# Sparse expert lookup of a graph network: groups of two gathers in a ring of eight, and a search spread over two tiles

## The chip, the cores and the metric

The kernel runs on one core of one Trainium2 chip. The metric is the device time in microseconds (us) of that core for one execution; less is better. TensorE is called PE here, VectorE DVE, ScalarE ACT, GpSimd POOL and SyncE SP.

## The reference, cut to what matters

The input x has 1250 rows of 512 floats. Four layers follow each other, each adding its result to x: a graph convolution with batch norm and GELU, a product-key expert lookup, a second graph convolution, and a binned dense layer. The change lies in the second layer, and in the start of the third that runs beside it:

```python
y = layernorm(x)                                  # 1250 x 512
q = (y @ Wq + bq).reshape(-1, 8, 128)             # 8 heads, two halves of 64
s1 = einsum(q[..., :64], keys[:, 0]); s2 = einsum(q[..., 64:], keys[:, 1])   # 256 scores each
s1t, i1 = top_k(s1, 8); s2t, i2 = top_k(s2, 8)
scores, best = top_k(all 64 sums of s1t and s2t, 8)
indices = the 8 pairs i1 * 256 + i2               # 64 rows of the tables for each row of y
vals = relu(einsum(y, w_down[indices])) * softmax(scores)
x = x + einsum(vals, w_up[indices])
```

Each of the 1250 rows of x so needs 64 rows of `w_down` and 64 of `w_up`. The host has put both tables side by side, so one gathered row has 1024 floats, 4096 bytes. All floats are fp32.

## The kernel before, in words

The rows of x are in NT = 10 tiles of 128 rows, one row to a partition. Before the lookup, the first graph layer runs; after it, the rest of the third layer and the sorted dense layer. The lookup and what runs beside it take most of the time.

**A slot.** For one tile and one of its 64 chosen experts, POOL issues an indirect DMA (line 476) that brings 128 table rows, one to each partition, into a slot of `big`. There are 16 slots. They are handled in groups of GS = 4, so NG = 16 groups a tile, and the ring has RING = 4 groups. A group passes four engines:

1. POOL waits until PE is done with the group that had these slots before (`grp_done`, line 471; also `val_ready`, line 470), then issues four gathers.
2. DVE waits until the group has landed, and forms four dot products of the `w_down` halves with y (line 956). After a drain it takes relu and multiplies by the softmax weight `prob` (line 961) for the four together, which gives `val`.
3. ACT makes four diagonal matrices `diag` from the identity, scaled by `val` (line 642).
4. PE multiplies them with the `w_up` halves and accumulates all 64 in one PSUM bank (line 1274). This sets `grp_done`. One fp32 matmul shows as two records.

**The search for the next tile** runs in between, in pieces tied to group numbers, written out by hand for each engine (`pieces` in the functions of PE, ACT and DVE). While tile i passes, DVE takes the norm of tile i + 1 (lines 822 to 840) at groups 1 and 2, PE transposes it at 2 (line 1221), PE computes the queries of four heads at group 3 and of four at 4 (line 1230), ACT copies them out at 4 and 5 (line 621), PE makes the scores of two heads in each of the groups 5 to 8 (line 1243), and DVE takes their eight best in groups 6 to 9, two heads at a time (lines 856 and 859). The pairs follow at 10 (lines 868 to 875), the row numbers are ready at 12 (line 902), the softmax at 14. Each engine does its list in order: an engine that waits in a piece does nothing for the ring meanwhile.

**The third layer's sums.** The finished tile i - 1 is added to x (line 922), normalized (line 840), and multiplied with the adjacency counts `AT` in 12 units (line 1253), two for each of the groups 10 to 15; DVE adds each unit to `outT` one group later (line 849). The units go alternately to two PSUM banks.

```python
pieces = {2: flip_y, 3: lambda i, p: queries(i, 0), 4: lambda i, p: queries(i, 1),
          5: lambda i, p: scores(i, 0), 6: lambda i, p: scores(i, 2), 7: lambda i, p: scores(i, 4),
          8: lambda i, p: scores(i, 6)}                      # PE
pieces = {1: root, 3: copy_yT, 4: lambda i: copy_q(i, 0), 5: lambda i: copy_q(i, 1), 12: exps}   # ACT
```

POOL and ACT run the tiles in loops of two tiles (ACT its first eight tiles, POOL all ten); DVE and PE have tiles 0, 1, 8 and 9 written out and a loop of two tiles for 2 to 7.

## Time and profile before

| what | value |
|---|---|
| time, median of 3 runs | 1517.33 us |
| lowest and highest run | 1516.46 and 1520.87 us |
| span of the profiled execution | 1598.9 us |
| time of the profiled execution apart from its span | not given; the span is the only one |
| mean granted clock of PE | 0.914 |
| instructions | 17228 |

The profile is of one execution, and its span is 81.6 us longer than the median of the runs without a profile. A row of a group gives line, engine, operation, the tiles written and read and how many; then its busy time, the mean of one in ns, and the idle time of the engine just before, with what ended it. In a timeline the first two numbers are the start and the duration in us; a merged row covers several instructions. A clock of 1.00 is 2.4 GHz, 0.50 is 1.2 GHz. The ends of matmuls are modelled.

### The profile page before, as it was taken

The numbers are of one execution on the slowest core, as the hardware profiler recorded it, in microseconds if no ns is written. First come the engines' busy times: TensorE is split into PE (matmuls) and PEld (weight loads), VectorE is DVE, ScalarE is ACT, GpSimd is POOL, SyncE is SP. The second block draws the span as 40 slices with busy tenths as digits, with TensorE's granted clock in tenths as the row PEclk, the third lists the DMA queues.
The fourth block names the chain that finished last, engine by engine and source line by source line (L and its number), as shares of the span: only waits on it lengthen the run. The fifth ranks groups of instructions, "written<-read, shape, count | busy, mean of one in ns | idle before, by whom it ended". The sixth has DMA issues, their size and how long they took to land.

```text
span 1598.9 us, 17228 instructions
## 1 busy us (share of the span) xinstructions
PE 1246.5 (78%) x3954; PEld 604.1 (38%) x3955; DVE 979.1 (61%) x3058; ACT 335.6 (21%) x910; POOL 829.4 (52%) x921
## 2 busy tenths in 40 slices
PE   4787789974877877797778878867887878788468
PEld 1333345542422433444334334343343433233233
DVE  4777771127497586684864866747758678555501
ACT  0111110024322223232221222221222222220011
POOL 5777700002567566565555665655656656763112
PEclk9999999985899999899888989988989999999779
DMA  9200000003889889898888898887998989986153
GB/s 350 87 0 0 0 0 0 1 0 118 307 305 349 298 325 345 281 324 320 302 302 301 300 336 301 316 322 261 361 338 291 354 301 350 373 327 243 72 184 125
DMA packets 105746, 378.51 MB, mean 237 GB/s; under 512 B 11824, under 2 KB 11826, under 8 KB 104536
## 3 DMA queue, kind: packets, MB, share of 16 engines
q0 software_dynamic: 94720, 343.40, 59.3%
q1 hardware_dynamic: 10968, 34.48, 5.8%
q8 instruction: 19, 0.31, 0.1%
q14 instruction: 39, 0.32, 0.1%
HBM read 359.53 MB, written 19.41 MB: 237 GB/s over the span
## 4 chain that ended last, share of the span: by engine, by line
PE 47%; DVE 19%; issue 12%; ACT 5%; DVEq 5%; another core or an unknown queue 5%; DMA 5%; POOL 2%; POOLq 0%; SPq 0%; ACTq 0%
PE tr L1274 20%; DVE big L956 8%; PE acc L1171 5%; PE acc L1230 4%; PE acc L1131 4%; PE acc L1253 3%; PE tr L1326 2%; DVE topi L859 2%; DMA big<-in_wdu,idx 2%; ACT diag L642 2%; PE tr L1302 2%; PE acc L1201 2%; PE acc L1243 2%; DVEq L730 2%
## 5 line engine op out<-in xcount | busy, mean ns | idle before, releaser
L476 POOL DMA_INDIRECT big<-in_wdu,idx x640 | 641.8, 1003 | 587.0 <-issue 583.1
L1274 PE MATMUL tr<-big,diag 128*128 128x512 f32 x1280 | 650.1, 656 | 190.2 <-ACT diag L642 98.1
L956 DVE CUSTOM_DVE_ANT_0 big<-big,y 128x512 f32<-128x512 f32 x640 | 405.3, 689 | 129.9 <-DMA big<-in_wdu,idx 100.9
L1274 PEld LDWEIGHTS tr<-big,diag 128*128 128x128 f32 x1280 | 255.8, 209 | 536.4 <-issue 402.2
L642 ACT ACTIVATE diag<-ident,val 128x128 f32<-128x128 f32 x640 | 204.6, 393 | 604.7 <-DVE val L961 342.1
L1131 PE MATMUL acc<-outT 128*128 128x512 f16 (+1 forms) x612 | 126.1, 345 | 33.0 <-POOL outT L461 14.7
L461 POOL TENSOR_SCALAR outT<-gt,big 128x128 f16<-128x128 f16 x153 | 130.2, 864 | 21.8 <-PE acc L1131 10.9
L856 DVE MAX8 top<-acc 128x8 f32<-128x256 f32 x160 | 61.2, 424 | 109.8 <-PE acc L1243 97.9
L736 DVE TENSOR_SCALAR outT<-big 128x1250 f16<-128x1250 f16 x204 | 110.3, 595 | 17.6 <-PE acc L1131 12.1
L1230 PE MATMUL acc<-yT,qk 128*128 128x128 f32 x640 | 86.5, 301 | 25.3 <-ACT qT L621 24.7
L1253 PE MATMUL acc<-AT,gt 128*128 (+2 forms) x240 | 97.4, 529 | 4.2 <-DVE gt L840 3.2
L849 DVE TENSOR_TENSOR outT<-outT,acc 128x512 f32<-128x512 f32 (+1 forms) x120 | 67.1, 586 | 54.4 <-PE acc L1253 37.6
L1230 PEld LDWEIGHTS acc<-yT,qk 128*128 128x128 f32 x640 | 85.0, 216 | 36.8 <-issue 19.3
L1131 PEld LDWEIGHTS acc<-outT 128*128 128x128 f16 x612 | 50.3, 98 | 106.7 <-DVE outT L736 36.8
L1171 PE MATMUL acc<-AT,big 128*128 128x512 f32 (+1 forms) x240 | 87.1, 526 | 3.8 <-DVEq L767 3.8
L1253 PEld LDWEIGHTS acc<-AT,gt 128*128 128x128 f32 x240 | 46.0, 195 | 56.1 <-issue 46.0
L859 DVE FIND_INDEX8 topi<-top,acc 128x8 uint32<-128x256 f32 x160 | 65.9, 424 | 1.2 <-issue 1.2
L1171 PEld LDWEIGHTS acc<-AT,big 128*128 128x128 f32 x240 | 46.7, 195 | 43.8 <-issue 39.7
L956 DVE DVE_READ_ACCUMULATOR2_ANT inner<- 128x1 f32 x640 | 52.6, 82 | 0.0
L621 ACT ACTIVATE qT<-acc,par 128x128 f32<-128x128 f32 x80 | 22.9, 369 | 139.1 <-remote 79.6
L1243 PE MATMUL acc<-qk,qT 64*128 64x256 f32 x320 | 47.5, 414 | 4.8 <-DVEq L861 4.4
L1079 DVE TENSOR_SCALAR pick<-x 128x1 int32<-128x1 f32 x14 | 2.2, 154 | 74.1 <-PE tr L1326 74.1
(217 smaller groups left out, 782.1 us busy)
## 6 DMA issues: line engine op xcount, KB each, us to landing
sorted_rows<-big SPq DMA_DIRECT2D x8, 1280.0 KB, 17.9
big<-in_wdu,idx POOLq DMA_INDIRECT x640
big<-in_we SPq DMA_DIRECT2D x8, 1024.0 KB, 14.0
x<-sorted_rows SPq DMA_DIRECT2D x14, 512.5 KB, 3.5
x<-in_x SPq DMA_DIRECT2D x1, 2304.0 KB
...
```

The costliest lines, as they stand in the source:

```text
L461: pool.tensor_scalar(k.ohd[c], k.tile_iota, k.dnow[:, c:c + 1], None, ALU.is_equal).then_inc(k.ohd_ready, 1)
L476: pool.indirect_dma_start(out=k.big[:, slot * 2 * D:(slot + 1) * 2 * D], out_offset=None, in_=k.wdu_d, in_offset=bass.IndirectOffsetOnAxis ...
L642: ins = act.activation(k.diag[:, ((g % 2) * GS + s) * P:((g % 2) * GS + s + 1) * P], k.ident[:, :], copy, scale=k.val[:, j:j + 1])
L736: dve.tensor_scalar(k.ohs[c][:, 0:N], k.iota[:, 0:N], k.now[:, c:c + 1], None, ALU.is_equal).then_inc(k.oh_ready, 1)
L859: ins = dve.max_index(k.topi[:, c * HK + h * 8:c * HK + h * 8 + 8], k.top[:, c * HK + h * 8:c * HK + h * 8 + 8], k.S[h % 2][c][:, 0:NK])
L956: dve.tensor_tensor_reduce(out=k.big[:, slot:slot + D], in0=k.big[:, slot:slot + D], in1=k.y[:, par * D:(par + 1) * D], scale=1.0, scalar=0.0,
L1131: ins = pe.matmul(k.acc[s][:, c0:c0 + n], k.ohd[b], k.ohs[b][:, c0:c0 + n], start=False, stop=False)
L1171: ins = pe.matmul(k.acc[s][:, c0:c0 + n], h[:, t * D + f * P:t * D + (f + 1) * P], k.AT[:, t * NPAD + c0:t * NPAD + c0 + n], start=(t == 0 ...
L1230: ins = pe.matmul(k.Q[:, b * P:(b + 1) * P], k.wq[:, f * H * P + h * P:f * H * P + (h + 1) * P], k.yT[:, f * P:(f + 1) * P], start=(f == 0 ...
L1243: ins = pe.matmul(k.S[h % 2][c][:, 0:NK], k.qT[half, h * P:(h + 1) * P], k.keys[half, h * NK:(h + 1) * NK], start=True, stop=True)
L1253: pe.matmul(k.G[u % 2][:, 0:n], k.h1[:, f * P:(f + 1) * P], k.AT[:, bass.ds(j * NPAD + c0, n)], start=True, stop=True).then_inc(k.g_ready, 1)
L1274: ins = pe.matmul(k.O[par], k.diag[:, c:c + P], k.big[:, slot:slot + D], start=(g == 0 and s == 0), stop=(g == NG - 1 and s == GS - 1))
```

## The change

It has four parts.

- **Two gathers a group.** GS is 2, NG is 32, RING is 8; there are still 16 slots. POOL no longer waits for DVE's semaphore, only for `grp_done`. There are four `diag` sets of two.
- **The softmax weight as the product's scale.** The dot product takes `prob` as its scale from memory, so the drain and the small product of line 961 are gone; ACT makes the diagonals with Relu in place of Copy.
- **The search in single steps over two tiles.** The search for tile j starts at step -14 (18 groups into tile j - 2) and ends at step 15 of tile j - 1. One step is one group of two. Queries are made for two heads at a time, scores and top eights for one. DVE takes a head two or more steps after PE made its scores. The search for tile 1 is shifted by 11 steps. y has three buffers.
- **Units one by one.** PE makes one unit in every second group from 8 on, in one PSUM bank in place of two, and DVE adds it three groups later. The transposed y moves to the bank of the queries. The norms of y and of the finished x are apart, with semaphores of their own.

All loops over tiles are written out: the engines have ten tiles of code each. The work after the lookup is unchanged.

```diff
-GS = 4
+GS = 2
 NG = HK // GS
-RING = 4
+RING = 8
+DB = 4
...
-UPP = 2
-FIRST_UNIT = NG * UPP - len(UNITS)
+NU = len(UNITS)
+
+
+Y_STATS, Y_NORM = -14, -11
+HEADS = (-4, -3, -1, 0, 2, 3, 5, 6)
+BEST, PLACE, CODES, MATCH, ROWS, INDEX, SOFTMAX = 8, 9, 10, 11, 12, 13, 15
+Y_ROOT, Y_FLIP, Y_COPY = -13, -10, -9
+QUERIES = (-9, -7, -5, -3)
+Q_COPY = (-8, -6, -4, -2)
+SCORES = (-6, -5, -3, -2, 0, 1, 3, 4)
+EXPS = 12
+LATE = 11
+
+
+X_ADD, X_STATS, X_ROOT, X_NORM = 4, 5, 6, 7
+UNIT_MM = [8 + 2 * u for u in range(NU)]
+UNIT_ADD = [11 + 2 * u for u in range(NU)]
+
+
+def at_search(i, g):
+
+    return [(i + a, g - NG * (a - 1) - (LATE if i + a == 1 else 0)) for a in (1, 2) if i + a < NT]
...
-    k.y = sb("y", 2 * D)
+    k.y = sb("y", 3 * D)
...
-    k.diag = sb("diag", 2 * GS * P)
+    k.diag = sb("diag", DB * GS * P)
...
-    k.YT = banks[0]
+    k.YT = banks[1]
...
-    def gather_tile(i, par):
-
+    for i in range(NT):
         pool.wait_ge(k.idx_ready, i + 1)
         for g in range(NG):
             r = g % RING
-
-            pool.wait_ge(k.val_ready, i * NG + g + 1)
             pool.wait_ge(k.grp_done, i * NG + g + 1)
-            pool.sem_inc(k.ring_free, 1)
             for s in range(GS):
                 j = g * GS + s
                 slot = r * GS + s
                 pool.indirect_dma_start(
                     out=k.big[:, slot * 2 * D:(slot + 1) * 2 * D], out_offset=None, in_=k.wdu_d,
-                    in_offset=bass.IndirectOffsetOnAxis(ap=k.idx[par][:, j:j + 1], axis=0),
+                    in_offset=bass.IndirectOffsetOnAxis(ap=k.idx[i % 2][:, j:j + 1], axis=0),
                 ).then_inc(k.landed[r], 16)
-
-    with pool.Fori(0, NT // 2) as pair:
-        gather_tile(pair * 2, 0)
-        gather_tile(pair * 2 + 1, 1)
...
+    def tile(i):
         for g in range(NG):
-            if g in pieces and (ahead or g == 1):
-                pieces[g](i + 1)
-            act.wait_ge(k.val_ready, i * NG + g + 1 + RING)
-            act.wait_ge(k.grp_done, i * NG + g - 1 + RING)
+            if i and g == X_ROOT:
+                x_root(i - 1)
+            for j, at in at_search(i, g):
+                search_step(j, at)
+            n = i * NG + g
+            act.wait_ge(k.inner_ready, n + 1)
+            act.wait_ge(k.grp_done, n + 1 - DB + RING)
             for s in range(GS):
                 j = g * GS + s
-                ins = act.activation(k.diag[:, ((g % 2) * GS + s) * P:((g % 2) * GS + s + 1) * P], k.ident[:, :],
-                                     copy, scale=k.val[:, j:j + 1])
+                c = (n % DB) * GS + s
+                ins = act.activation(k.diag[:, c * P:(c + 1) * P], k.ident[:, :], ACT.Relu,
+                                     scale=k.inner[:, j:j + 1])
             ins.then_inc(k.diag_ready, 1)
...
+    def x_add(i):
+        dve.wait_ge(k.grp_done, i * NG + NG + RING)
+        tile = k.x[:, i * D:(i + 1) * D]
+        dve.tensor_tensor(tile, tile, k.O[i % 2], ALU.add).then_inc(k.x2_done, 1)
...
+    def add_unit(j, u, bank):
+        f, c0, n = UNITS[u]
+        piece = k.agg1[:, f * NPAD + c0:f * NPAD + c0 + n]
+        dve.wait_ge(k.g_ready, j * NU + u + 1)
+        dve.tensor_tensor(piece, piece, k.G[bank][:, 0:n], ALU.add).then_inc(k.g_used, 1)
+
+    def top_head(i, h):
+        dve.wait_ge(k.s_ready, i * H + h + 1)
+        dve.sem_inc(k.s_seen, 1)
+        for c in range(2):
+            dve.max(k.top[:, c * HK + h * 8:c * HK + h * 8 + 8], k.S[h % 2][c][:, 0:NK])
+        dve.drain()
+        for c in range(2):
+            dve.max_index(k.topi[:, c * HK + h * 8:c * HK + h * 8 + 8],
+                          k.top[:, c * HK + h * 8:c * HK + h * 8 + 8], k.S[h % 2][c][:, 0:NK])
+        dve.drain().then_inc(k.topk_done, 1)
...
+    def tile(i):
         for g in range(NG):
-            if g == 1:
-                if behind:
-                    add_rows(i - 1, 1 - par)
-                norms(i + 1, ahead, behind)
-            if g == 2:
-                normed(i + 1, 1 - par, ahead, behind)
-            if ahead and g in pieces:
-                pieces[g](i + 1, 1 - par)
-            if behind and g > NG - len(UNITS) // UPP:
-                add_units(i - 1, (g - 1) * UPP - FIRST_UNIT, UPP)
-            if first_tile and g in (3, 4):
-                for t in range((g - 3) * (NT // 2), (g - 2) * (NT // 2)):
-                    loops = k.AT[:, t * NPAD + t * P:t * NPAD + (t + 1) * P]
-                    dve.tensor_tensor(loops, loops, k.ident[:, :], ALU.subtract)
-            if first_tile and g >= NG - FT:
+            if i and g == X_ADD:
+                x_add(i - 1)
+            if i and g == X_STATS:
+                x_stats(i - 1)
+            if i and g == X_NORM:
+                x_norm(i - 1)
+            if i and g in UNIT_ADD:
+                add_unit(i - 1, UNIT_ADD.index(g), 0)
+            if i > 1 and g + NG in UNIT_ADD:
+                add_unit(i - 2, UNIT_ADD.index(g + NG), 0)
+            for j, at in at_search(i, g):
+                search_step(j, at)
+            if i == 0 and g < NT:
+                loops = k.AT[:, g * NPAD + g * P:g * NPAD + (g + 1) * P]
+                dve.tensor_tensor(loops, loops, k.ident[:, :], ALU.subtract)
+            if i == 0 and g >= NG - FT:
                 dve.memset(k.agg1[:, (g - NG + FT) * NPAD:(g - NG + FT + 1) * NPAD], 0.0)
+            n = i * NG + g
             r = g % RING
-            use = i * (NG // RING) + g // RING
-            dve.wait_ge(k.landed[r], use * (16 * GS) + 16 * GS)
+            dve.wait_ge(k.landed[r], (n // RING + 1) * (16 * GS))
             for s in range(GS):
+                j = g * GS + s
                 slot = (r * GS + s) * 2 * D
-                dve.tensor_tensor_reduce(out=k.big[:, slot:slot + D], in0=k.big[:, slot:slot + D],
-                                         in1=k.y[:, par * D:(par + 1) * D], scale=1.0, scalar=0.0,
-                                         op0=ALU.mult, op1=ALU.add,
-                                         accum_out=k.inner[:, g * GS + s:g * GS + s + 1])
-            dve.drain()
-            dve.scalar_tensor_tensor(k.val[:, g * GS:(g + 1) * GS], k.inner[:, g * GS:(g + 1) * GS], 0.0,
-                                     k.prob[:, par * HK + g * GS:par * HK + (g + 1) * GS],
-                                     ALU.max, ALU.mult).then_inc(k.val_ready, 1)
-        if behind:
-            add_units(i - 1, len(UNITS) - UPP, UPP)
-
-    dve.sem_inc(k.val_ready, RING)
-    dve.sem_inc(k.g_used, 2)
-    search(0, 0)
+                ins = dve.tensor_tensor_reduce(
+                    out=k.big[:, slot:slot + D], in0=k.big[:, slot:slot + D],
+                    in1=k.y[:, (i % 3) * D:(i % 3 + 1) * D],
+                    scale=k.prob[:, (i % 2) * HK + j:(i % 2) * HK + j + 1], scalar=0.0, op0=ALU.mult, op1=ALU.add,
+                    accum_out=k.inner[:, j:j + 1])
+            ins.then_inc(k.inner_ready, 1)
...
+    def queries(i, c):
         pe.wait_ge(k.yT_done, i + 1)
-        pe.wait_ge(k.qT_done, i * H + 4 * half)
-        for b in range(4):
-            h = 4 * half + b
+        pe.wait_ge(k.qT_done, i * H + 2 * c)
+        for h in (2 * c, 2 * c + 1):
             for f in range(FT):
-                ins = pe.matmul(k.Q[:, b * P:(b + 1) * P], k.wq[:, f * H * P + h * P:f * H * P + (h + 1) * P],
+                ins = pe.matmul(k.Q[:, (h % 4) * P:(h % 4 + 1) * P],
+                                k.wq[:, f * H * P + h * P:f * H * P + (h + 1) * P],
                                 k.yT[:, f * P:(f + 1) * P], start=(f == 0), stop=(f == FT - 1))
         ins.then_inc(k.q_ready, 1)
 
-    def scores(i, h0):
-        for h in (h0, h0 + 1):
-            pe.wait_ge(k.qT_done, i * H + h + 1)
-            if h >= 2:
-                pe.wait_ge(k.topk_done, i * H + h - 1)
-            else:
-                pe.wait_ge(k.topk_done, i * H)
-            for c in range(2):
-                half = slice(64 * c, 64 * c + 64)
-                ins = pe.matmul(k.S[h % 2][c][:, 0:NK], k.qT[half, h * P:(h + 1) * P],
-                                k.keys[half, h * NK:(h + 1) * NK], start=True, stop=True)
-            ins.then_inc(k.s_ready, 1)
-
-    def units(j, u0, n_units):
-
+    def scores(i, h):
+        pe.wait_ge(k.qT_done, i * H + h + 1)
+        pe.wait_ge(k.topk_done, max(i * H + h - 1, 0))
+        for c in range(2):
+            half = slice(64 * c, 64 * c + 64)
+            ins = pe.matmul(k.S[h % 2][c][:, 0:NK], k.qT[half, h * P:(h + 1) * P],
+                            k.keys[half, h * NK:(h + 1) * NK], start=True, stop=True)
+        ins.then_inc(k.s_ready, 1)
+
+    def unit(j, u, bank, ahead):
+        f, c0, n = UNITS[u]
         pe.wait_ge(k.ht_ready, j + 1)
-        for u in range(u0, u0 + n_units):
-            f, c0, n = UNITS[u]
-            pe.wait_ge(k.g_used, j * len(UNITS) + u + 1)
-            pe.matmul(k.G[u % 2][:, 0:n], k.h1[:, f * P:(f + 1) * P], k.AT[:, bass.ds(j * NPAD + c0, n)],
-                      start=True, stop=True).then_inc(k.g_ready, 1)
-
-    pieces = {2: flip_y, 3: lambda i, p: queries(i, 0), 4: lambda i, p: queries(i, 1),
-              5: lambda i, p: scores(i, 0), 6: lambda i, p: scores(i, 2), 7: lambda i, p: scores(i, 4),
-              8: lambda i, p: scores(i, 6)}
-
-    def search(i, par):
-        for g in (2, 3, 5, 4, 6, 7, 8):
-            pieces[g](i, par)
-
-    def tile(i, par, ahead, behind):
+        pe.wait_ge(k.g_used, max(j * NU + u - ahead, 0))
+        pe.matmul(k.G[bank][:, 0:n], k.h1[:, f * P:(f + 1) * P], k.AT[:, j * NPAD + c0:j * NPAD + c0 + n],
+                  start=True, stop=True).then_inc(k.g_ready, 1)
+
+    def search_step(i, at):
+        if at == Y_FLIP:
+            flip_y(i)
+        if at in QUERIES:
+            queries(i, QUERIES.index(at))
+        if at in SCORES:
+            scores(i, SCORES.index(at))
+
+    def tile(i):
         for g in range(NG):
-            if ahead and g in pieces:
-                pieces[g](i + 1, 1 - par)
-            if behind and g >= NG - len(UNITS) // UPP:
-                units(i - 1, g * UPP - FIRST_UNIT, UPP)
-            pe.wait_ge(k.diag_ready, i * NG + g + 1)
+            for j, at in at_search(i, g):
+                search_step(j, at)
+            if i and g in UNIT_MM:
+                unit(i - 1, UNIT_MM.index(g), 0, 0)
+            n = i * NG + g
+            pe.wait_ge(k.diag_ready, n + 1)
             for s in range(GS):
                 slot = ((g % RING) * GS + s) * 2 * D + D
-                c = ((g % 2) * GS + s) * P
-                ins = pe.matmul(k.O[par], k.diag[:, c:c + P], k.big[:, slot:slot + D],
+                c = ((n % DB) * GS + s) * P
+                ins = pe.matmul(k.O[i % 2], k.diag[:, c:c + P], k.big[:, slot:slot + D],
```

## Rows read from the trace of the kernel before

**Rows 1.** The page, part 1: busy time of each engine over the whole span.
```profile
span 1598.9 us, 17228 instructions
...
PE 1246.5 (78%) x3954; PEld 604.1 (38%) x3955; DVE 979.1 (61%) x3058; ACT 335.6 (21%) x910; POOL 829.4 (52%) x921
```

**Rows 2.** Windows: stretch, us, busy PE, PEld, DVE, ACT, POOL, clock, DMA share, GB/s.
```profile
612.00:718.00 106.00, 86.13 (x254) 42.67 (x255) 75.89 (x253) 29.48 (x83) 63.45 (x65) 0.92 0.89 316
...
1254.00:1360.00 106.00, 86.97 (x259) 41.69 (x260) 75.84 (x253) 27.49 (x80) 65.08 (x65) 0.94 0.92 331
...
384.00:1446.00 1062.00, 843.55 (x2428) 405.09 (x2428) 723.01 (x2419) 272.83 (x791) 641.81 (x640) 0.91 0.88 316
```

**Rows 3.** The page, part 3: the queue that carries the gathers.
```profile
q0 software_dynamic: 94720, 343.40, 59.3%
```

**Rows 4.** The page, part 5: the lookup's groups, with the idle time before them.
```profile
L476 POOL DMA_INDIRECT big<-in_wdu,idx x640 | 641.8, 1003 | 587.0 <-issue 583.1
L1274 PE MATMUL tr<-big,diag 128*128 128x512 f32 x1280 | 650.1, 656 | 190.2 <-ACT diag L642 98.1
L956 DVE CUSTOM_DVE_ANT_0 big<-big,y 128x512 f32<-128x512 f32 x640 | 405.3, 689 | 129.9 <-DMA big<-in_wdu,idx 100.9
```

**Rows 5.** Timeline of gathers: start, duration, idle before; the last two are tile 9's.
```profile
606.02 0.95 POOL L476 DMA_INDIRECT big<-in_wdu,idx  x1 [0.30 <-issue]
...
648.76 0.95 POOL L476 DMA_INDIRECT big<-in_wdu,idx  x1 [5.41 <-issue]
...
1341.71 0.95 POOL L476 DMA_INDIRECT big<-in_wdu,idx  x1 [0.77 <-issue]
...
1431.70 0.95 POOL L476 DMA_INDIRECT big<-in_wdu,idx  x1 [0.30 <-issue]
```

**Rows 6.** Windows of 5 us in tiles 1 and 2: full and starved DMA engines.
```profile
590.00:595.00 5.00, 5.00 (x12) 2.18 (x12) 2.77 (x12) 1.28 (x4) 3.60 (x4) 1.00 1.02 416
...
645.00:650.00 5.00, 5.00 (x18) 2.20 (x17) 1.17 (x4) 1.86 (x7) 0.95 (x1) 1.00 0.39 155
```

**Rows 7.** Timeline: group 3 of tile 2 through the ring.
```profile
617.11 0.95 POOL L476 DMA_INDIRECT big<-in_wdu,idx  x1 [0.30 <-issue]
...
623.98 0.69 DVE L956 CUSTOM_DVE_ANT_0 big<-big,y 128x512 f32<-128x512 f32 x1 [2.31 <-DMA big<-in_wdu,idx]
...
626.60 0.16 DVE L961 SCALAR_TENSOR_TENSOR val<-inner,prob 128x4 f32<-128x4 f32 x1
...
626.80 1.28 ACT L642 ACTIVATE diag<-ident,val 128x128 f32<-128x128 f32 x4 [2.39 <-DVE val L961]
...
630.62 3.60 PE L1274 MATMUL tr<-big,diag 128*128 128x512 f32 x8
```

**Rows 8.** Waits between 384 and 1446 us: who for whom, total us, times, longest us.
```profile
DVE top L856 <- PE acc L1243: 87.3, 18, 10.0
ACT qT L621 <- remote: 79.6, 8, 12.3
...
DVE outT L849 <- PE acc L1253: 30.7, 32, 3.0
```

**Rows 9.** Timeline of DVE in tile 3: two heads of one piece, and their second waits.
```profile
760.99 0.76 DVE L856 MAX8 top<-acc 128x8 f32<-128x256 f32 x2
...
763.03 0.76 DVE L856 MAX8 top<-acc 128x8 f32<-128x256 f32 x2 [0.30 <-issue]
```

**Rows 10.** Timeline of PE: queries, a unit pair, and a group at the lower clock.
```profile
607.04 1.40 PE L1253 MATMUL acc<-AT,gt 128*128 128x512 f32 x4
...
627.05 3.73 PE L1230 MATMUL acc<-yT,qk 128*128 128x128 f32 x32
...
732.73 6.38 PE L1274 MATMUL tr<-big,diag 128*128 128x512 f32 x8 [5.72 <-ACT diag L642]
```

**Rows 11.** Groups with shapes apart: the score product and ScalarE's table loads.
```profile
L961 DVE SCALAR_TENSOR_TENSOR val<-inner,prob 128x4 f32<-128x4 f32 x160 | 26.2, 164 | 23.3 <-issue 11.6
...
L626 ACT ACT_TABLE_LOAD x10 | 12.8, 1283 | 0.2
```

More of the change, by code:

```diff
@@ new lines, in softmax, with search_step @@
+        dve.drain()
+    def search_step(i, at):
+        if at == Y_STATS:
+            y_stats(i)
+        if at == Y_NORM:
+            y_norm(i)
+        if at in HEADS:
+            top_head(i, HEADS.index(at))
+        if at == BEST:
+            best()
+        if at == PLACE:
+            place()
+        if at == CODES:
+            codes()
+        if at == MATCH:
+            match()
+        if at == ROWS:
+            rows()
+        if at == INDEX:
+            index(i)
+        if at == SOFTMAX:
+            softmax(i)
@@ L984, in dve_program @@
-    add_units(NT - 1, 0, len(UNITS))
+    dve.drain()
+    for at in range(Y_STATS, -LATE):
+        search_step(1, at)
+    for i in range(NT):
+        tile(i)
+    for u in range(NU):
+        if UNIT_ADD[u] >= NG:
+            add_unit(NT - 2, u, 0)
+    x_add(NT - 1)
+    x_stats(NT - 1)
+    x_norm(NT - 1)
+    for u in range(NU):
+        add_unit(NT - 1, u, u % 2)
     dve.drain()
@@ L1280, in pe_program @@
     pe.sem_inc(k.grp_done, RING)
-    search(0, 0)
+    for at in range(Y_FLIP, SCORES[-1] + 1):
+        search_step(0, at)
     for i in range(1, NT):
@@ L1284, in pe_program @@
     pe.wait_ge(k.x1_done, NT)
[L1285 to L1295 removed]
+    for i in range(NT):
+        tile(i)
+    for u in range(NU):
+        unit(NT - 1, u, u % 2, 0 if u == 0 else 1)
+    pe.wait_ge(k.g_used, NT * NU)
     pe.wait_ge(k.x2_done, NT)
```

176 lines of the change are left out of this document (69 added, 107 removed).

## The prediction

> **What bounds the kernel now.** I read the page's totals first: no engine is full over the span of 1598.9 us, PE with 78% comes nearest [rows 1]. Then the windows over the lookup, which holds two thirds of the span: 1062 us in which PE is busy 843.6, DVE 723.0, POOL 641.8 and the DMA engines 88% [rows 2]. A tile takes 106 or 107 us in them, whether it lies in the written-out loops or not. So the question is what each engine would need for one tile if nothing held it up.
>
> POOL: a gather takes 1.003 us on average [rows 4], and the next starts 0.30 us later when nothing holds POOL [rows 5]. 64 x 1.303 = 83.4 us a tile. DMA: the gathers' queue moved 343.40 MB [rows 3], 0.537 MB each; full engines move 416 GB/s [rows 6], so 1.29 us a gather and 82.6 us a tile. PE: 86.1 us busy in a tile at a granted clock of 0.92 [rows 2], about 79 us at the full one. DVE: 75.9 us busy [rows 2], plus what the busy time leaves out, a 0.30 us wait after each drain of a head [rows 9], 16 of them a tile: about 81 us. Four engines need 79 to 83 us each, and the tile takes 106. From 384 to tile 9's first gather at 1341.7 [rows 2, 5] nine tiles take 957.7 us, 106.4 each. POOL's part of that is 83.4, so it stands 23.0 us a tile waiting for a slot. A long stand is seen at 648.76, after 5.41 us [rows 5], and the DMA engines were at 0.39 share and 155 GB/s around it [rows 6]. The kernel is bound by its hand-overs, not by an engine.
>
> Two hand-overs matter. **The ring's own length:** group 3 of tile 2 is fully issued at 618.06; its products start at 623.98, 5.9 us later, with DVE waiting for the DMA; the value is ready at 626.76, 2.8 us later; the diagonals take 1.28 us, and the matmuls 3.60 us, which here start late [rows 7]. With 5.0 us to issue four gathers and 0.3 us to start again, a group needs 5.0 + 5.9 + 2.8 + 1.3 + 3.6 + 0.3 = 18.9 us from first issue to reuse. The ring gives it four groups' time at POOL's pace, 4 x 4 x 1.303 = 20.8 us. Less than 2 us of lateness on any engine stops POOL. **The search:** DVE waits 87.3 us for score matmuls, up to 10.0 us at a time, 30.7 us for units, and ACT 79.6 us for the queries, up to 12.3 us [rows 8]. Each far exceeds 2 us. The 12.3 us ones end on a release that the profile can't name.
>
> **The change, part by part.** Groups of two: 2.5 to issue, 5.9 to land, about 1.5 for two products, 0.7 for two diagonals, 1.8 for the matmuls, 0.3: 12.7 us of the same 20.8, so 8.1 us of slack in place of 1.9. The cost is 16 more starts of a group on each engine. No row shows that start alone; from 0 to the 0.30 us of a drained wait [rows 9], 0 to 4.8 us a tile. I take 1.6, because nothing is drained there any more.
>
> The value product: 26.2 us over 160 [rows 11], 2.6 us a tile of DVE, goes, and with it a hand-over on each group's way. The scale read from memory instead of a constant isn't in the trace. The same product at 0.689 us [rows 4] bounds it below; above I allow a tenth, 0.07 x 64 = 4.5 us a tile. I take nothing: 512 elements pass either way. DVE so needs 81 - 2.6 + 1.6 = 80 us, up to 88 at both upper bounds. Relu in place of Copy on ACT: at worst a table load of 1.283 us [rows 11] around each change of function, a few us a tile, under ACT's idle time (29.5 of 106 us busy [rows 2]); that cover is ample.
>
> The search in steps: queries in four parts of 16 matmuls, half of a record row of 3.73 us [rows 10], so PE is away from the ring for 1.9 us at a time, less than the slack. DVE takes one head of 2.04 us [rows 9] at a time, two steps after PE made it, so the 87.3 us of waits should mostly go; likewise the 30.7 us for units, now added three groups later. PE's unit waits for the add of the one before, because one bank is left; that add, 0.6 us, lies beside ACT's diagonals. What becomes late next is DVE's uneven list: steps 0 to 9 hold five heads (10.2 us), ten products of two (about 14) and some 7.5 us of norms, adds and pairs, 31.7 us against the 10 x 2.6 = 26.1 that POOL takes; it falls 5.6 us behind, within 8.1, and catches up in steps 16 to 27, which hold little. PE's steps 23 to 30 (units, queries and scores together) are about as tight. The softmax and row numbers are ready at steps 15 and 13, well ahead of their first use. POOL's extra waits are on `grp_done` alone, two gathers queued behind each.
>
> **The sum.** Tile 9 has no search at all: its 64 gathers run from 1341.7 to 1432.7 [rows 5], 90.9 us, 7.5 us over POOL's 83.4. I take that residue and 1.5 us for the uneven list: 92.4 us a tile. Nine tiles save 9 x (106.4 - 92.4) = 126 us, tile 9 about 2, the rest of the program nothing: its search, tail and layers issue the same work. The profiled span would be 1598.9 - 128 = 1471 us.
>
> The runs without a profile are 81.6 us shorter than that span, and where these lie I can't see. If they are spread in proportion, the saving is 128 x 1517.33 / 1598.9 = 121 us and the time 1396. If they all lie in the nine tiles (the 79.6 us of unnamed releases [rows 8] suggest it), an unprofiled tile already takes 97.3 us, the saving is 9 x 4.9 + 2 = 46, and the time 1471. The truth is between; I take 1430.
>
> A rule speaks against the change. Mean gathers take 1.003 us, usual ones 0.95 [rows 4, 5], so 0.05 us each is lost to something now. The Trainium skill (SBUF - State Buffer, "Who interferes with whom") says that a DVE instruction with two SBUF inputs contends with a GpSimd one that reads SBUF, and that one blocks wholly. The row shows only a mean of 0.05 us for it, if it is that. By the rule the denser stream of products could block POOL more often; that is the second rival.
>
> **The rivals.** (1) The residue goes too: all engines run at their need, 84 us a tile; 9 x 22.4 = 202 us of the span, 191 in proportion, 1326. For: four needs of 79 to 83. Against: four engines so evenly filled never all run freely, and tile 9 doesn't. Chance 0.07. (2) POOL is held up: if half of the products' 0.689 us fell on each gather, 64 x 0.34 = 22 us a tile would take back the 23.0 that POOL stood, and the time stays near 1517. Against: the 0.05 us now. Chance 0.05. (3) Slower: PE's clock. After 5.72 us of idleness a group took 6.38 us instead of 3.60 [rows 10, 7], at the lower level. Now PE gets 1.8 us of work at a time and waits twice as often. Its 79 us become the bound of 106 below a mean clock of 0.74; at 0.70 a tile is 113 us, 9 x 6.6 x 0.95 = 56 us more, 1573. Against: shorter stands, with more work per us than now, and 0.92 today. Chance 0.09. In the TensorE: Matmul & The Clock Gate page of the Trainium skill ("What's actually happening") the throttled state is the default and activity releases it; by that, steadier work helps. (4) The waits only move, from heads to other steps: 100 us a tile, 1517.3 - 9 x 6.4 x 0.95 = 1463; that lies in my forecast.
>
> **The numbers.** The forecast, with (4), has 0.79. A measurement of this kernel tells 0.3%, 4.6 us, from no change. Faster 0.86 (0.79 + 0.07), same 0.05, slower 0.09. The range goes from 1365 (88.5 us a tile in proportion) to 1500 (the span's excess all in the tiles and DVE near 88 with waits left), which leaves out (1), (2) and (3).
>
> **What would show it.** Right: POOL's idle time falls from 587 us by some 130, beside a gather mean still near 1.0; DVE's wait for scores falls under 20 us; the lookup's windows show 360 GB/s or more, PE's clock 0.92 or better, a tile of about 92 us. Wrong: DVE's group of line 956 with a mean over 0.75; gathers over 1.1 us; a clock under 0.8; DVE waits on steps 0 to 9 that fill the ring.

## The result and the profile after

The changed kernel takes **1434.89 us** (median of four runs, 1433.85 to 1435.95) against 1517.78 us for the kernel before, four runs on the same chip: a ratio of 0.9455, 95% interval 0.9438 to 0.9471. The forecast was 1430 in a range of 1365 to 1500.

The profiled execution of the changed kernel lasts 1434.2 us. Its totals, its gather queue and its costliest groups (busy us, mean ns | idle us before, and the releaser of most of it):

```profile
span 1434.2 us, 16301 instructions
...
PE 1201.3 (84%) x3954; PEld 565.9 (39%) x3955; DVE 989.3 (69%) x2906; ACT 345.7 (24%) x914; POOL 857.4 (60%) x921
...
q0 software_dynamic: 94720, 343.40, 62.6%
...
L493 POOL DMA_INDIRECT big<-in_wdu,idx x640 | 670.1, 1047 | 396.2 <-DVE idx L931 180.7
L1302 PE MATMUL tr<-big,diag 128*128 128x512 f32 x1280 | 612.0, 607 | 85.9 <-ACT diag L666 85.6
L992 DVE CUSTOM_DVE_ANT_0 big<-big,y,prob 128x512 f32<-128x512 f32 x640 | 451.1, 747 | 76.1 <-DMA big<-in_wdu,idx 63.8
...
L883 DVE MAX8 top<-acc 128x8 f32<-128x256 f32 x160 | 60.9, 422 | 69.9 <-PE acc L1272 68.7
```

These answer to [rows 1, 3, 4] and the first of [rows 8]. The ring's matmuls wait 85.9 us in place of 190.2, the value product's group is gone, and POOL's idle time is 396.2 in place of 587.0; 180.7 of it is the wait for the first row numbers, ahead of the lookup. (A second profile of the kernel before, below, has 167.7 and 509.0 for these two.) Two rows went the wrong way: a gather takes 1.047 us in place of 1.003, and a product 0.747 in place of 0.689.

A window of 700 us, nearly eight steady tiles, and four gathers of the timeline; the first and the last are the first gathers of tiles 0 and 9:

```profile
480.00:1180.00 700.00, 631.73 (x1949) 293.05 (x1948) 596.08 (x1863) 217.90 (x614) 529.07 (x501) 1.00 0.99 376
```
```profile
384.25 1.22 POOL L493 DMA_INDIRECT big<-in_wdu,idx  x1 [180.70 <-DVE idx L931]
...
580.60 1.43 POOL L493 DMA_INDIRECT big<-in_wdu,idx  x1 [0.95 <-PE tr L1302]
...
614.59 1.87 POOL L493 DMA_INDIRECT big<-in_wdu,idx  x1 [0.74 <-PE tr L1302]
...
1188.38 1.01 POOL L493 DMA_INDIRECT big<-in_wdu,idx  x1 [0.30 <-issue]
```

Nine tiles take 1188.38 - 384.25 = 804.1 us, **89.35 us each**. PE's granted clock is 1.00, the DMA engines are busy 99% of the time at 376 GB/s, and POOL issues nearly without a pause: its waits for a slot are now about a microsecond, as in the second row. The third row is a gather that itself took twice the usual time; that is taken up with the second SBUF operand below. The same shows in the waits between 384 and 1280 us (who for whom, total us, times, longest us):

```profile
ACT diag L666 <- DVE inner L992: 466.1, 245, 3.7
...
POOL big L493 <- issue: 171.7, 563, 0.5
...
DVE top L883 <- PE acc L1272: 55.9, 26, 7.0
POOL big L493 <- PE tr L1302: 43.8, 76, 1.7
```

POOL's "issue" time is the fixed 0.30 us between gathers, 563 times and never over 0.5; its waits for the ring's matmuls last 1.7 us at most. In [rows 5] one lasted 5.41.

### The profile page after: what moved, and what is told of

It reads as the page before. It is cut to its first block, busy times and chain, and to the rows that moved or that the text cites. A ratio compares the mean times of both kernels' runs of the same rounds, so it can differ in the third digit from the quotient of the medians.

```text
span 1434.2 us, 16301 instructions
## 1 busy us (share of the span) xinstructions
PE 1201.3 (84%) x3954; PEld 565.9 (39%) x3955; DVE 989.3 (69%) x2906; ACT 345.7 (24%) x914; POOL 857.4 (60%) x921
## 4 chain that ended last, share of the span: by engine, by line
PE 47%; DVE 28%; issue 6%; DVEq 6%; DMA 5%; POOL 3%; ACT 3%; POOLq 0%; SPq 0%; ACTq 0%
PE tr L1302 17%; DVE big L992 11%; PE acc L1204 6%; PE acc L1262 5%; PE acc L1164 5%; PE acc L1280 4%; DVE topi L886 4%; POOL big L493 3%; PE tr L1351 3%; DVE top L883 2%; DMA big<-in_wdu,idx 2%; PE tr L1327 2%; PE acc L1234 2%; DVEq L752 2%; DVE outT L758 1%
## 5 line engine op out<-in xcount | busy, mean ns | idle before, releaser
L493 POOL DMA_INDIRECT big<-in_wdu,idx x640 | 670.1, 1047 | 396.2 <-DVE idx L931 180.7
L1302 PE MATMUL tr<-big,diag 128*128 128x512 f32 x1280 | 612.0, 607 | 85.9 <-ACT diag L666 85.6
L992 DVE CUSTOM_DVE_ANT_0 big<-big,y,prob 128x512 f32<-128x512 f32 x640 | 451.1, 747 | 76.1 <-DMA big<-in_wdu,idx 63.8
L1302 PEld LDWEIGHTS tr<-big,diag 128*128 128x128 f32 x1280 | 229.5, 190 | 391.3 <-issue 216.6
L666 ACT ACTIVATE diag<-ident,inner 128x128 f32<-128x128 f32 x640 | 219.5, 394 | 466.1 <-DVE inner L992 466.1
L1164 PE MATMUL acc<-outT 128*128 128x512 f16 (+1 forms) x612 | 125.8, 344 | 33.5 <-POOL outT L482 15.5
L758 DVE TENSOR_SCALAR outT<-big 128x1250 f16<-128x1250 f16 x204 | 109.9, 592 | 17.9 <-PE acc L1164 12.3
L1280 PE MATMUL acc<-AT,gt 128*128 128x512 f32 (+1 forms) x240 | 108.3, 537 | 12.5 <-DVE outT L877 7.3
L1262 PEld LDWEIGHTS acc<-yT,qk 128*128 128x128 f32 x640 | 80.6, 199 | 20.8 <-issue 18.8
L1262 PE MATMUL acc<-yT,qk 128*128 128x128 f32 x640 | 81.8, 283 | 1.8 <-ACT qT L637 1.0
L1280 PEld LDWEIGHTS acc<-AT,gt 128*128 128x128 f32 x240 | 41.4, 191 | 75.5 <-issue 71.3
L1272 PE MATMUL acc<-qk,qT 64*128 64x256 f32 x320 | 57.9, 440 | 4.4 <-DVEq L888 4.4
```

Source lines behind the costliest of these rows:

```text
L493: pool.indirect_dma_start(out=k.big[:, slot * 2 * D:(slot + 1) * 2 * D], out_offset=None, in_=k.wdu_d, in_offset=bass.IndirectOffsetOnAxis ...
L666: ins = act.activation(k.diag[:, c * P:(c + 1) * P], k.ident[:, :], ACT.Relu, scale=k.inner[:, j:j + 1])
L758: dve.tensor_scalar(k.ohs[c][:, 0:N], k.iota[:, 0:N], k.now[:, c:c + 1], None, ALU.is_equal).then_inc(k.oh_ready, 1)
L992: ins = dve.tensor_tensor_reduce(out=k.big[:, slot:slot + D], in0=k.big[:, slot:slot + D], in1=k.y[:, (i % 3) * D:(i % 3 + 1) * D], scale= ...
L1164: ins = pe.matmul(k.acc[s][:, c0:c0 + n], k.ohd[b], k.ohs[b][:, c0:c0 + n], start=False, stop=False)
L1262: ins = pe.matmul(k.Q[:, (h % 4) * P:(h % 4 + 1) * P], k.wq[:, f * H * P + h * P:f * H * P + (h + 1) * P], k.yT[:, f * P:(f + 1) * P], sta ...
```

## The experiments

All runs in one table. "us/tile" is the start of tile 9's first gather less that of tile 0's, over 9. "Stands" is what POOL waits beyond 0.30 us between gathers, per tile, in those nine tiles. Ratios are to runs of the kernel before on the same chip; its medians there were 1518.54 (beside e2 to e4), 1520.18 (e5 to e8), 1517.88 (e9 to e11) and 1516.39 (e12). They lie 4 us apart, so a difference of a few us between rows of different chips is uncertain by about as much.

| run | us, median (lowest to highest) | ratio [95% interval] | us/tile | gather, us | product, us | stands |
|---|---|---|---|---|---|---|
| before, profile shown | 1517.78 (1516.46-1520.87) | 1 | 106.4 | 1.003 | 0.689 | 22.7 |
| e1_base | 1517.9 (one) | | 98.35 | 0.998 | 0.689 | 14.9 |
| e2_scale | 1516.97 (1510.72-1521.84) | 0.9987 [0.9968, 1.0005] | 97.7 | 1.013 | 0.748 | 13.4 |
| e3_pairs | 1480.75 (1478.6-1481.56) | 0.9757 [0.9724, 0.9789] | 94.2 | 1.051 | 0.690 | 7.2 |
| e4_pairs_scale | 1460.79 (1458.34-1463.65) | 0.962 [0.9583, 0.9656] | 92.2 | 1.023 | 0.748 | 7.1 |
| e8_pairs_scale_unrolled | 1445.25 (1443.32-1446.4) | 0.9501 [0.9452, 0.9551] | 90.2 | 1.033 | 0.748 | 4.4 |
| **after** | 1434.89 (1433.85-1435.95) | 0.9455 [0.9438, 0.9471] | 89.35 | 1.047 | 0.747 | 2.3 |
| e5_after_fours | 1512.26 (1508.12-1518.42) | 0.9957 [0.9932, 0.9982] | 97.1 | 1.007 | 0.747 | 13.2 |
| e11_unrolled | 1495.04 (1494.58-1498.41) | 0.9846 [0.9808, 0.9884] | 95.6 | 1.000 | 0.689 | 12.0 |
| e6_after_unit_scale | 1418.41 (1416.79-1420.52) | 0.9331 [0.9281, 0.9381] | 87.3 | 1.020 | 0.689 | 2.2 |
| e7_after_narrow | 1388.71 (1384.97-1390.66) | 0.9138 [0.9089, 0.9187] | 83.45 | 0.961 | 0.282 | 2.4 |
| e9_one_score | 1435.05 (1431.68-1435.83) | 0.9446 [0.9412, 0.948] | 88.5 | 1.043 | 0.746 | 1.8 |
| e10_y_in_psum | 1429.25 (1428.41-1432.2) | 0.9412 [0.9376, 0.9448] | 87.8 | 0.953 | 0.741 | 7.3 |
| **e12_weight_on_act** | 1419.45 (1417.23-1420.43) | 0.9357 [0.9329, 0.9385] | 86.6 | 0.952 | 0.681 | 6.1 |

### The kernel before, profiled again

The profile on which the prediction rests had a span 81.6 us over the timed runs. Run e1_base is the same kernel.

> The kernel before, unchanged, profiled once more. The first profile of it had a span of 1598.9 us against runs of 1517 us, with 79.6 us of ACT waits at line 621 on a release that the profile couldn't name; the changed kernel's profile (span 1434.2 us) has neither. Theory A (the excess belongs to recording this kernel): the span is again near 1599 us and the 79.6 us are there. Theory B (that one execution was disturbed): the span is near 1517 us, a tile takes about 97 us in the windows, and POOL's idle time before line 476 is some 80 us below 587 us.

The new profile's span is 1516.1 us (timeline rows first, then the page's group of gathers and waits between 384 and 1250 us):

```profile
383.32 1.22 POOL L476 DMA_INDIRECT big<-in_wdu,idx  x1 [179.87 <-issue]
...
1268.45 0.94 POOL L476 DMA_INDIRECT big<-in_wdu,idx  x1 [0.78 <-issue]
...
1350.30 0.94 POOL L476 DMA_INDIRECT big<-in_wdu,idx  x1 [0.31 <-issue]
```
```profile
L476 POOL DMA_INDIRECT big<-in_wdu,idx x640 | 638.8, 998 | 509.0 <-issue 504.8
```
```profile
ACT qT L621 <- PE acc L1230: 69.1, 18, 5.3
...
DVE top L856 <- PE acc L1243: 45.0, 15, 5.4
```

It agrees with the timed runs to 2 us. Nine tiles take 885.1 us, 98.35 each, and the releases that the first profile couldn't name don't appear. So the first profile was of an unusual execution, and its 81.6 us lay mainly in the nine tiles: 9 x (106.4 - 98.35) = 72. Another 8 us lay in tile 9: from its first gather to the end of its last, 1268.45 to 1351.24, it takes 82.8 us here, where the first profile had the 90.9 from which the prediction took its residue. The waits for queries and scores were there in ordinary executions too, but at most 5.4 us long rather than 12.3. What disturbed that one execution stays open. From here on "before" means e1_base; the change is worth 9 x (98.35 - 89.35) = 81 of the 83 us measured.

### One part at a time: weight as scale, groups of two

```diff
 e2_scale: before, and
-  tensor_tensor_reduce(..., scale=1.0, ...); dve.drain(); scalar_tensor_tensor(k.val, ...)
+  tensor_tensor_reduce(..., scale=k.prob[:, j], ...)      # diagonals: Relu(ident * inner)
 e3_pairs: before, and
-GS = 4; RING = 4
+GS = 2; RING = 8; DB = 4       # search pieces stay at every fourth gather
 e4_pairs_scale: both
```

> Part two alone on the kernel before: the softmax weight as the product's scale, Relu, no drain and no product of the four values. Groups of four and the old search stay. Ring-length theory: the way of a group through the ring shortens by about 0.25 us of 18.9, but each product takes 0.747 us in place of 0.689 as in the changed kernel, four of them 0.23 us more; so nothing, 1512 to 1522 us. Rival (the value product and its hand-over cost much): below 1500 us.

> Part one alone on the kernel before: groups of two, eight in the ring, four diag sets of two; each piece of the search still stands at the same place of the tile, two heads at once, units in pairs on two banks, the value product kept. Ring-length theory: the slack grows from 1.9 to about 8 us, which covers most stands but not the 10 us waits for scores; about half of the gain, 1465 to 1490 us. Search theory: the waits of the search stay whole, so nothing or less than 10 us, 1507 to 1520 us.

> Parts one and two on the kernel before, without the search in single steps over two tiles. What is left to the changed kernel's 1435 us is the worth of the steps. Ring-length theory: 1460 to 1485 us, so the steps are worth 25 to 50 us. Search theory: 1500 to 1520 us, so the steps are worth 65 to 85 us.

The product in the kernel with the scale alone:

```profile
L957 DVE CUSTOM_DVE_ANT_0 big<-big,y,prob 128x512 f32<-128x512 f32 x640 | 443.3, 748 | 125.7 <-DMA big<-in_wdu,idx 106.8
```

Alone, the scale is worth nothing that can be measured: the interval holds 1. What the value product and its drain gave, the longer product (+59 ns) took. Groups of two alone save 37.8 us (1518.54 - 1480.75) and halve POOL's stands, 14.9 to 7.2. With them the gather gets longer, 0.998 to 1.051 us, 3.4 us a tile; that takes back nearly half of what the stands give. On top of them the scale saves another 20.0 us. Groups of two pay for 32 drains and value products a tile without it, and DVE's busy time falls from 1003.4 to 989.7 us between these two runs. But the stands are the same (7.2 and 7.1); of the 2.0 us that a tile loses, 64 x (1.051 - 1.023) = 1.8 are shorter gathers. Why the gathers are shorter with the longer product wasn't tested.

### The loops over pairs of tiles

In e4_pairs_scale two tiles are longer than the others, tile 4 (98.4 us) and tile 6 (97.1 us); the rest take 90 or 91. These two follow a jump back of the loop on DVE and PE. Two rows of its DVE timeline, the last adds of tile 5 and the first product of tile 6:

```profile
946.89 0.99 DVE L851 TENSOR_TENSOR outT<-outT,acc 128x512 f32<-128x512 f32 x2 [0.91 <-PE acc L1254]
952.40 0.75 DVE L959 CUSTOM_DVE_ANT_0 big<-big,y,prob 128x512 f32<-128x512 f32 x1 [4.52 <-issue]
```

At its tile 6 DVE stands 4.52 us for nothing that the profile can name. The trace of before has the same stand at its tile 4, and it could have been read before predicting:

```profile
825.35 0.74 DVE L956 CUSTOM_DVE_ANT_0 big<-big,y 128x512 f32<-128x512 f32 x1 [4.63 <-issue]
```

```diff
 e8_pairs_scale_unrolled and e11_unrolled (on before), on POOL, ACT, DVE and PE:
-    with dve.Fori(1, NT // 2 - 1) as pair:
+    for pair in range(1, NT // 2 - 1):
```

> Groups of two and the product scale on the kernel before, as in e4, with the old search, and all loops over tiles of PE, DVE, ACT and POOL written out. In e4 tiles 4 and 6, which begin with the loop's jump back on DVE and PE, take 98.4 and 97.1 us, the others 90.0 to 91.4, and DVE stands 4.3 to 5.0 us at the jump. If the jump is the cause: both tiles take 90 to 91 us and the time is 1443 to 1450 us. If something else comes round every two tiles: they stay at 97 to 98 and the time within 4 us of 1461.

> The kernel before with all loops over tiles written out and nothing else. Jump theory: tiles 4 and 6, 100.7 and 101.7 us in e1, come to the others' 97, and the slack of 2 us covers none of the two jumps: 6 to 16 us less, 1503 to 1513. Rival (only the long ring shows the jump, as the old search hides it): no difference that can be told, 1515 to 1521.

In all five traces that have the loops (before, e1 to e4) DVE stands 4.2 to 5.4 us ahead of the first product of tiles 4 and 6, and of no other tile that the loop runs. With the loops written out e4's tiles 4 and 6 take 90.7 and 90.1 us; these two give back 14.7 of the 15.5 us between the two runs. On the kernel before, writing the loops out saves 22.8 us (1517.88 - 1495.04) with nothing else changed, more than the 6 to 16 expected. Tiles 4 and 6 lose 6.5 and 6.1 us there (100.7 to 94.2, 101.7 to 95.6); tile 0, with no jump of DVE's or PE's before it, loses 5.9 as well (101.7 to 95.8), and what that is stays open. So a part of the change that the prediction gave nothing is worth 15 to 23 us, of which 13 to 15 are shown to lie at the jumps. The loops of all four engines were written out together; which engine's jump costs the time wasn't separated. The Trainium skill (Runtime: NRT & Kernel Launch, "Instruction fetch mechanics") says that a taken branch breaks the sequential prefetch of instructions. The rows agree with a stall at the jump, though they don't name instruction fetch as its cause.

### What the steps over two tiles are worth

Between e8 and after lies what is left of the change: the rearranged search, the units one by one, and POOL's dropped wait for DVE, which weren't taken apart. 1445.25 to 1434.89 is 10 us; by the ratios, 0.9501 and 0.9455 on two chips, it is 7, and the two intervals overlap. The tile in the traces went from 90.2 to 89.35, 8 us in nine. The other way round, the changed kernel with groups of four again:

```diff
-GS = 2; RING = 8; DB = 4
+GS = 4; RING = 4; DB = 2; NSTEP = 32; PER = NSTEP // NG   # two search steps before each group
```

> The changed kernel with part one undone: groups of four, four in the ring, two diag sets of four; the single steps keep their places, two of them ahead of each group; product scale and written-out tiles stay. Ring-length theory: the ring's slack is 2 us again, less than what two steps together take on DVE (two heads 4 us), so POOL stands some 8 us a tile and the time is 1490 to 1515 us. Search theory: with the waits for scores gone the group size matters little, 1440 to 1460 us.

```profile
POOL big L495 <- PE tr L1307: 137.8, 69, 5.7
DVE top L886 <- PE acc L1276: 79.5, 44, 11.5
```

It takes 1512.26 us: without groups of two, scale, steps and written-out loops together are worth 8 us, less than the 23 us of the loops alone on the kernel before, so steps and scale together cost 17 us there (1512.26 - 1495.04). Most of that is in tile 0, 107.2 us against 95.8 in e11, which is 11 of the 17; why it is there wasn't looked into. Tiles 1 to 8 take 95.9 against 95.6, so there steps and scale bring nothing and cost next to nothing. POOL is back to waits of up to 5.7 us for the ring, and stands 13.2 us a tile, more than the 8 expected. Groups of two carry the change: 38 us on the old structure, 77 on the new one. The steps show no gain in a ring without slack.

### What bounds the changed kernel

e6_after_unit_scale is the changed kernel with the constant 1.0 as the product's scale, so the softmax weight is left out. e7_after_narrow computes the products over 64 of the 512 columns.

```diff
 e6:  -  scale=k.prob[:, ...]            +  scale=1.0
 e7:  -  k.big[:, slot:slot + D], k.y[:, ... + D]
      +  k.big[:, slot:slot + 64], k.y[:, ... + 64]
```

> The changed kernel with the products' scale 1.0 from the instruction in place of the softmax weight from memory; the softmax weight is left out of the result, Relu stays. DVE's product goes back from 0.747 to 0.689 us, 3.7 us a tile. If POOL's issuing bounds the changed kernel (it stands only 2.1 us a tile), the time stays within 4 us of 1435. If DVE does, it falls by 20 to 35 us, to 1400 to 1415 us.

> The changed kernel with products over 64 of the 512 columns; seven eighths of each dot product are left out. DVE has some 25 us a tile less to do. It measures how far POOL's gathers are stretched by DVE beside them: the mean gather is 1.047 us, the usual one 0.95. If products with two operands in SBUF hold POOL up, as rival two and the port rule have it, the mean falls to 0.96 or less, a tile to 82 to 83 us (then the DMA engines bound it) and the time to 1375 to 1390 us. If not, the mean stays at 1.04 to 1.05, and the time within 6 us of 1435.

```profile
L493 POOL DMA_INDIRECT big<-in_wdu,idx x640 | 652.9, 1020 | 395.6 <-DVE idx L931 180.7
...
L992 DVE CUSTOM_DVE_ANT_0 big<-big,y 128x512 f32<-128x512 f32 x640 | 414.7, 689 | 82.0 <-DMA big<-in_wdu,idx 69.5
```
```profile
L493 POOL DMA_INDIRECT big<-in_wdu,idx x640 | 614.8, 961 | 394.9 <-DVE idx L931 178.8
...
L992 DVE CUSTOM_DVE_ANT_0 big<-big,y,prob 128x64 f32<-128x64 f32 x640 | 155.8, 282 | 297.8 <-DMA big<-in_wdu,idx 286.0
```
```profile
480.00:1180.00 700.00, 663.02 (x1995) 301.33 (x1994) 375.86 (x1923) 233.24 (x644) 518.80 (x542) 1.00 1.02 404
```

The first fence is of e6, the other two of e7. The scale operand costs 16 us of the time, between what the two theories of e6 gave (at most 4, and 20 to 35): DVE is no separate bound here, it acts through the gathers. In both runs the tile follows the gather's length. e6: 64 x (1.047 - 1.020) = 1.7 us of the 2.0 us that a tile lost. e7: 64 x (1.047 - 0.961) = 5.5 of 5.9. POOL is the bound of the changed kernel, at 64 x (1.047 + 0.30) = 86.2 us and 2.3 of stands (88.5 of the 89.35; over the nine tiles alone the mean gather is 1.055, which makes it 89.0). In these two runs shorter products go with shorter gathers; it is no general rule, since e3 has products of 0.690 us and gathers of 1.051. With narrow products the tile is 83.45 us and the DMA engines move 404 GB/s, close to the 416 of [rows 6]. Their share reads 0.99 at 376 GB/s, 1.00 at e12's 389 and 1.02 at 404: it doesn't tell that they can move no more, and e7 shows that they aren't the bound of the changed kernel.

### Is it the second SBUF operand?

e9_one_score frees two PSUM banks (one pair of score banks, a head every second step, the row numbers three steps later) and is the control; e10_y_in_psum has ScalarE copy y there, so that the product has one operand in SBUF.

```diff
 e9:   -  k.S[h % 2][c]     +  k.S[0][c]        # HEADS every second step
 e10 (on e9):
+    act.activation(k.YP[i % 2], k.y[:, ...], copy)         # 16 steps ahead, once a tile
-    in1=k.y[:, ...]
+    in1=k.YP[i % 2]
```

> The changed kernel with one pair of score banks in place of two: scores of a head at steps -6, -4 to 8, its top eights two steps later, row numbers at 16 and softmax at 18 in place of 13 and 15. It is the control for the next run, which needs the two banks. The spacing of the heads is even now. Expected by every theory: within 6 us of 1435; a few us more if tile 1's row numbers, now at step 27, come too late for POOL.

> As e9, but the products read y from a PSUM bank (ACT copies it there from SBUF once a tile at step 16, 0.6 us); the gathered rows still come from SBUF. The products stay 512 columns wide. Port theory (a DVE instruction with two operands in SBUF holds up POOL's descriptor work): the mean gather falls from 1.047 us towards the 0.961 of e7, a tile to 84 to 86 us, the time to 1390 to 1415 us. Rival (e7 was faster only because DVE had less to do, or because the ring was fed better): the mean gather stays at 1.03 to 1.05 and the time within 6 us of e9.

```profile
L496 POOL DMA_INDIRECT big<-in_wdu,idx x640 | 609.8, 953 | 447.6 <-DVE idx L941 190.7
...
L1004 DVE CUSTOM_DVE_ANT_0 big<-big,acc,prob 128x512 f32<-128x512 f32 x640 | 446.9, 741 | 43.7 <-DMA big<-in_wdu,idx 32.3
```
```profile
POOL big L496 <- PE tr L1314: 94.7, 111, 2.5
```

The control takes the changed kernel's time (its tiles are 0.85 us shorter, its first gather starts 4.1 us later). With y in PSUM a product is about as long as in the control (0.741 against 0.746), and yet the gather falls from 1.043 to 0.953. Of 640 gathers 298 take over 0.97 us in e9, and 10 in e10. The second operand in SBUF is what stretches them. The long gather of the first section is a neighbour of another instruction, the comparison of the search for the next tile, which also reads two operands from SBUF:

```profile
614.42 1.23 DVE L917 TENSOR_TENSOR pick<-posf,iota8h 128x1024 f16<-128x1024 f16 x1
```
```profile
709.95 1.23 DVE L927 TENSOR_TENSOR pick<-posf,iota8h 128x1024 f16<-128x1024 f16 x1
...
710.41 1.58 POOL L496 DMA_INDIRECT big<-in_wdu,idx  x1 [1.20 <-PE tr L1314]
```

The first row is of the changed kernel, the other two of e10, where this comparison stays as it was: the gather beside it still takes 1.58 us, and eight of the ten long ones are such.

The gather went as the port theory had it, but the time gains only 5.8 us where that theory expected 20 or more: of the 64 x 0.090 = 5.8 us a tile that POOL gets free, 5.5 return as waits for a slot (stands 1.8 to 7.3). Another bound lies close behind, at 87.8 us a tile.

### Weight on ScalarE: a version that beats both

```diff
 e12 (on e10):
+    act.activation(k.val[:, j:j+1], k.inner[:, j:j+1], Relu, scale=k.prob[:, w:w+1])   # per slot
+    act.drain()
-    act.activation(k.diag[...], k.ident, Relu, scale=k.inner[:, j:j+1])
+    act.activation(k.diag[...], k.ident, copy, scale=k.val[:, j:j+1])
-    tensor_tensor_reduce(..., scale=k.prob[...])
+    tensor_tensor_reduce(..., scale=1.0)
```

> This is the run with y read from PSUM, and in addition ScalarE applies the softmax weight: for each slot one activation of a single element (Relu of the inner product times the probability), a drain for the group, and then the scaled identity with that element as its scale; the product on VectorE has the constant 1.0 as its scale again. Theory A (with the gathers no longer stretched it is VectorE, 741 ns a product, that sets the 87.8 us of a tile): the product falls to about 0.69 us, VectorE gets 64 x 0.05 = 3.3 us a tile free, the tiles come to 84.5 to 86 us and the time to 1400 to 1415 us. Theory B (TensorE's 614 us in 680 and the descent through the ring, which gets some 0.5 us a group longer by the added activations, set the tile): the product falls as in A, but the tiles stay within 0.6 us of 87.8 and the time within 6 us of 1429; if the longer descent decides, it rises above 1435.

```profile
L1010 DVE CUSTOM_DVE_ANT_0 big<-big,acc 128x512 f32<-128x512 f32 x640 | 408.3, 681 | 50.6 <-DMA big<-in_wdu,idx 39.4
L675 ACT ACTIVATE val<-inner,prob 128x1 f32<-128x1 f32 x640 | 152.5, 286 | 273.7 <-DVE inner L1010 272.9
```
```profile
500.00:1180.00 680.00, 631.43 (x1928) 287.01 (x1928) 555.84 (x1851) 341.08 (x1132) 480.74 (x506) 1.00 1.00 389
```

1419.45 us, below the changed kernel's interval (0.9357 [0.9329, 0.9385] against 0.9455 [0.9438, 0.9471]): the fastest kernel here that does all of the work. It falls between what the two theories expected. DVE got 64 x 0.060 = 3.8 us a tile free and the tile lost 1.2. VectorE was part of what set e10's pace, and not alone: PE is busy 631 of 680 us here, 93%, and the DMA engines all the time. What holds the last 3 us over e7's 83.45 wasn't separated.

## Why the prediction came out right, step by step

**What bounds the kernel.** Right. The ring's hand-overs bound the kernel before, and POOL, not yet full, was their victim: groups of two, which change no engine's work but add to it, cut its stands from 14.9 to 7.2 us a tile and the time by 38 us. The slack sum ("1.9" against "8.1" us) names the decisive part, and e5 confirms it from the other side.

**Groups of two, 1.6 us of starts.** In busy time the 16 more starts a tile cost DVE nothing and ACT 1.3 us: from e2 to e4 DVE goes from 989.9 to 989.7 us in all, ACT from 337.2 to 350.3. What they cost in idle time wasn't separated. What the term left out is larger, the 3.4 us a tile by which the gathers got longer in e3.

**The value product, -2.6 us, and the scale, "I take nothing".** The second was the wrong end of the bound. The product went from 0.689 to 0.747, 64 x 0.058 = 3.7 us a tile, near the upper bound of 4.5; "512 elements pass either way" was no reason. e6 prices it at 16 us of the whole time. With groups of four it cancels the value product's gain, within what can be measured. The mark of a mean over 0.75 was only just not reached.

**Relu at nothing.** Right: a scaled identity takes 394 ns (391 in e1), and in e2, where Relu comes in with groups unchanged, ACT is busy 337.2 us against 336.6.

**"Whether it lies in the written-out loops or not".** Wrong, worth 15 us on the pairs and 23 on the kernel before. The two windows that it was judged by [rows 2] were chosen 106 us wide, and lie in tiles with no jump back before them; from first gather to first gather the tiles of that trace take 102.8 to 113.5 us, and the longest is tile 4. A stall that comes once in two tiles has to be looked for at the jump.

**The search in steps.** DVE's waits for scores were to fall under 20 us and measure 55.9 over the lookup, against 45.0 in the ordinary execution of before. That step failed. The waits are at the first heads of a search: of the eight heads for tile 3, DVE waits 3.03, 1.26 and 1.63 us for the first three and not at all for the other five. Here are the queries and the scores on PE, and the first head on DVE:

```profile
562.02 1.95 PE L1262 MATMUL acc<-yT,qk 128*128 128x128 f32 x16
...
565.62 0.70 PE L1272 MATMUL acc<-qk,qT 64*128 64x256 f32 x4
```
```profile
566.48 0.76 DVE L883 MAX8 top<-acc 128x8 f32<-128x256 f32 x2 [3.03 <-PE acc L1272]
```

PE makes them in the steps that also hold queries and units, the ones that the prediction called tight; two steps of distance don't cover what PE is behind there. Yet it cost little: POOL's stands still fell from 4.4 (e8) to 2.3. The steps bring 7 to 10 us, the smallest part of the gain. e9, with one pair of score banks and evenly spaced heads, takes the same time, so the second pair isn't needed.

**92.4 us a tile; measured 89.35.** The sum's 83.4 for POOL became 86.2, since the gathers were stretched from 1.003 to 1.047. The residue of 7.5 us taken from tile 9 and 1.5 for the uneven list became 2.3 of stands. The residue belonged to the unusual execution: in e1 tile 9 takes 82.8 us, with nothing over POOL's need. Rival 1, all engines at their need and 84 us a tile, wasn't reached either.

**The conversion to unprofiled time.** The prediction had two, 1396 and 1471, and took the middle. e1 shows that the second was the true reading: an ordinary tile takes 98.35 us, its text said 97.3. By that reading alone the forecast would have been 36 us too slow, made up of 9 x 3.05 = 27 us for the tile after and 9 x 1.05 = 9 us for the tile before. So 1430 is near 1434.89 because a tile better than forecast made up for a conversion that was too favourable: two errors of opposite sign. That the number came so close is luck; that the ring's slack would bring a large gain is not. The range held both. The saving predicted in POOL's idle time, 130 us from 587, came as 113 from the ordinary 509.

**The port rule (rival 2).** Its mechanism is real and its size a small one. The rule of the Trainium skill (SBUF - State Buffer, "Who interferes with whom") that a DVE instruction with two SBUF inputs contends with a GpSimd one that reads SBUF agrees with e10: one operand moved to PSUM, and the gather falls from 1.043 to 0.953. The price is 0.09 us a gather, 5.8 us a tile, not the 22 us of the rival, and the change raised it by only 64 x (1.047 - 0.998) = 3.1 us a tile.

**PE's clock (rival 3).** It went the other way: 0.95 to 1.00 in the steady tiles (e1 and after, the same windows), and [rows 2] had 0.92. PE's waits for diagonals in the lookup are 85.6 us in all, the longest 5.4. Rival 4 (waits only move, 1463) describes e4 and e8 better than the finished change.

## What to carry to other kernels

In a ring, write down the time from first issue to reuse and compare it with what the ring gives; if the slack is smaller than the stalls of any engine in the path, make the groups smaller before anything else is moved. Each part's worth depends on that: the scale brought 0 us with groups of four and 20 with two, and the steps gained 7 to 10 us with two and, together with the scale, nothing with four. Where the profiled span is well over the timed runs, profile once more before summing durations; here 72 of the 82 us of excess lay in the nine tiles that were being judged, and 8 in the tile that served as the measure of what would be left.

## What the runs showed that wasn't expected

- A scale read from memory makes a 128x512 product-and-sum on VectorE 58 ns longer (0.689 to 0.747; 0.741 to 0.681 the other way in e12).
- An indirect gather's issue on GpSimd takes 0.94 to 0.95 us undisturbed. It gets longer beside VectorE instructions with two operands in SBUF: 1.86 to 1.87 us beside the search's comparison of 1.23 us in seven tiles of the changed kernel. The mean over all falls from 1.043 to 0.953 when one operand of the products lies in PSUM.
- At a loop's jump back VectorE stands 4.5 to 5.2 us in the rows of before and e4, and in e4 the tile takes 7 us longer. Written-out loops have no such stand.
- One execution in the profiler took 1598.9 us where others of the same kernel take 1516, at a granted clock of 0.91 over the lookup, with releases that it couldn't name.
